# A mixture-of-experts stage: the second product's weights become the moving side, in three passes, and 32 rows of four experts share one pass over column quarters

## The reference

```python
h = jnp.einsum('ech,efh->ecf', buf, expert_w1)
x1, x2 = jnp.split(h, 2, axis=-1)
out = jnp.einsum('ecf,ehf->ech', x1 * jax.nn.silu(x2), expert_w2)
y = out[se, jnp.clip(rank, 0, CAPACITY - 1)]
y = jnp.where(valid[:, None], y * sw[:, None].astype(y.dtype), 0.0)
combined = jnp.zeros((T, H), x.dtype).at[st].add(y)
```

## Time and profile before

| | before |
|---|---|
| median of 3 runs | 1949.8 us (1949.53 to 1949.85) |
| span of the profiled execution | 1947.9 us |
| PE busy over the span | 1899.4 us (98%) |
| DVE, ACT, POOL busy | 1046.4, 829.4, 934.5 us |
| granted clock of PE, mean | 0.989 |
| stage 3 | from about 1238.5 us to the end |

### The profile page before, as it was taken

One profiled execution on the slowest core, in us unless ns is written; L12 is line 12 of the kernel. 1 busy time (PEld: TensorE's weight loads), 2 busy tenths in 40 slices (PEclk: granted clock), 3 DMA queues, 4 the chain that ended last, 5 costly groups with the idle time before them and its releaser, 6 DMA issues.

```text
span 1947.9 us, 35918 instructions
## 1 busy us (share of the span) xinstructions
PE 1899.4 (98%) x12384; PEld 1693.5 (87%) x12384; DVE 1046.4 (54%) x2262; ACT 829.4 (43%) x1661; POOL 934.5 (48%) x667
## 2 busy tenths in 40 slices
PE   7999999999999999999999999889999999999998
PEld 5888888888888887688777887789999999999998
DVE  7877777777777776776667777311221221212211
ACT  6666666666666665553354443111111111211211
POOL 5666666566666662056656666462222222222222
PEclk9999999999999999999999999889999999999999
DMA  6211111111111102121001110567778787787785
GB/s 220 68 37 34 36 33 36 35 45 41 36 36 33 53 11 94 46 75 54 23 23 44 44 33 1 183 177 252 249 258 265 244 272 255 251 273 246 266 266 152
DMA packets 104279, 233.83 MB, mean 120 GB/s; under 512 B 20676, under 2 KB 84891, under 8 KB 96032
## 3 DMA queue, kind: packets, MB, share of 16 engines
q1 hardware_dynamic: 79648, 220.48, 32.4%
q0 software_dynamic: 24576, 12.69, 4.4%
HBM read 194.56 MB, written 78.45 MB: 140 GB/s over the span
## 4 chain that ended last, share of the span: by engine, by line
PE 58%; another core or an unknown queue 1%; DVE 1%; issue 0%; ACT 0%; POOLq 0%; ACTq 0%; POOL 0%; DVEq 0%
PE bank L1870 32%; PE bank L82 19%; PE bank L1149 4%; PE bank L2046 1%; PE bank L2009 1%; PE bank L1647 1%; DVE b_h_low L1429 0%; DVE early L1526 0%; POOLq L2081 0%; DVE c_gT L1965 0%; DVE b_g L1513 0%; DVE b_g L1515 0%; ACT early L1332 0%; ACT b_h_high L1326 0%
## 5 line engine op out<-in xcount | busy, mean ns | idle before, releaser
L1965 DVE TENSOR_TENSOR c_gT<-bank,c_sil 128x480 f32<-128x480 f32 x128 | 84.2, 658 | 559.3 <-PE bank L1870 516.0
L1847 POOL DMA_INDIRECT slots<-b_row,b_index x224 | 249.9, 1116 | 197.8 <-issue 116.3
L1986 POOL DMA_INDIRECT out_rows<-c_y,c_x x96 | 134.2, 1398 | 341.3 <-DMA out_rows<-c_y,c_x 213.7
L1870 PE MATMUL bank<-c_gT,c_w 128*128 128x160 f32 x1536 | 226.9, 304 | 12.4 <-DVE c_gT L1965 10.5
L1870 PEld LDWEIGHTS bank<-c_gT,c_w 128*128 128x128 f32 x1536 | 214.1, 192 | 14.1 <-DVE c_gT L1965 9.3
L1870 PE MATMUL bank<-c_xT,early 128*128 128x160 f32 x1536 | 221.8, 301 | 1.5 <-issue 0.9
L1870 PE MATMUL bank<-c_xT,c_w 128*128 128x160 f32 x1536 | 219.2, 299 | 0.0
L1870 PEld LDWEIGHTS bank<-c_xT,early 128*128 128x128 f32 x1536 | 213.8, 192 | 1.5 <-issue 1.4
L1870 PEld LDWEIGHTS bank<-c_xT,c_w 128*128 128x128 f32 x1536 | 211.4, 190 | 0.0
L1942 ACT ACTIVATE c_sil<-bank 128x480 f32<-128x480 f32 x128 | 73.0, 570 | 287.5 <-PE bank L1870 275.3
L439 POOL TENSOR_TENSOR last_row<-last_row,a_e 128x256 f32<-128x256 f32 x33 | 54.4, 1648 | 129.4 <-DVE a_e L695 127.7
(11 more groups left out here) (317 smaller groups left out, 4940.0 us busy)
## 6 DMA issues: line engine op xcount, KB each, us to landing
c_w<-in_e2T SPq DMA_DIRECT2D x64, 768.0 KB
c_w<-in_e1T SPq DMA_DIRECT2D x32, 1536.0 KB
early<-in_e1T SPq DMA_DIRECT2D x31, 1536.0 KB
slots<-a_fill SPq DMA_DIRECT2D x16, 642.0 KB
c_x<-slots SPq DMA_DIRECT2D x48, 200.6 KB
a_x_in<-in_x SPq DMA_DIRECT2D x32, 128.0 KB, 2.0
xT_tiles<-a_xT SPq DMA_DIRECT2D x32, 128.0 KB
swaT_tiles<-a_swaT SPq DMA_DIRECT2D x32, 128.0 KB
```

The source lines that it names most:

```text
L1847: pool.indirect_dma_start(out=T["slots"], out_offset=bass.IndirectOffsetOnAxis(ap=index[:, t, k:k + 1], axis=0), in_=row[:, t, :], in_offs ...
L1870: return nc.tensor.matmul(out, lhsT, rhs, start=first, stop=last, skip_group_check=True)
L1965: dve.tensor_tensor(flat(gT[p][:, g * H:(g + 1) * H, :]), psum[2 + 2 * g][:, 0:H * CAP], flat(sil[:, g * H:(g + 1) * H, :]), ALU.mult).the ...
L1986: pool.indirect_dma_start(out=T["out"], out_offset=bass.IndirectOffsetOnAxis(ap=token, axis=0), in_=y[q % 2][:, h, :], in_offset=None, bou ...
```

## The change

The edits are all in stage 3, but for one call in stage 2's SP function.

- **Rows.** The 160 rows of an expert are split into a block of 128 (`x`, eight buffers) and a rest of 32 (`x_rest`: the rests of four experts, a quad, stand in the four quarters of one tile's partitions; two such tiles). Their row numbers are loaded once more by themselves (`token_rest`).
- **Second product of the 128 rows.** `gT` is the stationary side now and `w2` moves past it, 256 columns, so that the result has the rows in the partitions, and `yT`, its copies and `turn_y` are gone. It is computed by `mm_split`: ACT makes the high halves of `w2` (1536 columns) and `gT` (twice 384), and DVE the low ones. That is 18 passes of 256 columns.
- **Second product of the rests.** `down_rest` runs once for a quad, as plain float32: for each of 6 slices, four products with 32 stationary columns and 256 moving ones, one for each expert, that write the four quarters of one bank's partitions.
- **Order.** PE's order is `turn_x(n)`, `up` group 1 of n - 1, `up` group 0 of n, `down(n - 1)`, and `down_rest` at every fourth expert. `w2` and `gT` have eight buffers. `w1` and then `w2` of expert n are issued one behind the other, once the first product of expert n - 2 has ended; the rows of expert n wait for the adds of expert n - 8.
- **Adds.** One indirect transfer of 128 rows and one of 32 for each expert; the adds of a quad's first expert wait until the quad's rests are done, which DVE does at the second expert of the next quad.
- **Start and loop.** `first_weights` issues `w1` of experts 0 and 1 and `w2` of expert 0 in stage 2, after its last product with `linT`. POOL issues the 32 scatters that are left in one row ahead of any add. Eight experts are written out ahead of the loop, whose body has eight (6 turns), and eight behind it.

```diff
-    w1 = [buf["early"][:, 0:DC * 2 * FFN].rearrange("p (k f) -> p k f", k=DC), sb("w1_1", [P, DC, 2 * FFN])]
-    w2 = [sb(f"w2_{p}", [P, FC, D]) for p in range(2)]
-    x = [first_rows(buf)] + [sb(f"x{q}", [HALF, 2, ROW])[:] for q in range(1, 4)]
+    w1 = [sb(f"w1_{p}", [P, DC, 2 * FFN]) for p in range(2)]
+    w2_first = sb("w2_0", [P, FC, D])
+    x = [sb(f"x{q}", [P, ROW]) for q in range(RING)]
+    early = [buf["early"][:, p * FC * D:(p + 1) * FC * D].rearrange("p (k d) -> p k d", k=FC) for p in range(2)]
+    w2 = [w2_first[:]] + early + [sb(f"w2_{q}", [P, FC, D])[:] for q in range(3, RING)]
+    w2s = [split(f"w2s{p}", [P, FC, D]) for p in range(2)]
     sil = sb("sil", [P, FC, CAP])
-    gT = [sb(f"gT{p}", [P, FC, CAP]) for p in range(2)]
+    gT = [sb(f"gT{q}", [P, FC, CAP]) for q in range(RING)]
+    gTs = [split(f"gTs{p}", [P, FC, P]) for p in range(2)]
...
+    def experts(eng, step):
+        for n in range(RING):
+            step(n, n, 0)
+        with eng.Fori(1, E // RING - 1) as i:
+            for q in range(RING):
+                step(i * RING + q, q, i)
+        for n in range(E - RING, E):
+            step(n, n % RING, E // RING - 1)
...
+    def first_weights(sp):
+        sp.wait_ge(B("lin_mm"), 4 * CHUNKS)
+        for n in range(2):
+            load_w1(sp, n, n)
+        load_w2(sp, 0, 0)
...
-            wait_past(sp, S("added"), (n - 3) * 32)
+            elif q % QUAD == 0:
+                sp.wait_ge(S("y_rest"), quad_of(q, i) - 1)
+                for j in range(QUAD):
+                    load_rest(n + j, q + j)
+            wait_past(sp, S("added"), (n - RING + 1) * 32)
+            sp.dma_start(x[q][:], slot_rows(T, n, 0, P)).then_inc(S(f"x_in{q}"), 16)
+            sp.dma_start(token_rest[q][:], slot_rows(T, n, P, REST)[:, D + E - 1:ROW]).then_inc(S(f"token_in{q}"), 16)
+            if not first or n >= 2:
+                sp.wait_ge(S("h_mm"), (n - 1) * 4)
+                load_w1(sp, n, q % 2)
+            if not first or n >= 1:
+                if not first:
+                    wait_past(sp, S("rest_mm"), quad_of(q, i) - 1)
+                load_w2(sp, n, q)
...
+        def step(n, q, i):
             p = q % 2
             act.wait_ge(S("xT_mm"), n + 1)
             wait_past(act, S("h_mm"), (n - 1) * 4)
-            act.copy(flat(xT[p][:]), psum[0][:, 0:DC * CAP]).then_inc(S("xT"), 1)
+            by_block = psum[0][:, 0:2 * DC * P].rearrange("p (s k t) -> p s k t", s=2, k=DC)
+            act.copy(xT[p][:, :, 0:P], by_block[:, 0])
+            act.copy(xT[p][:, :, P:CAP], by_block[:, 1, :, quarter(q % QUAD)]).then_inc(S("xT"), 1)
-                   .then_inc(S("sil"), 1)
+                silu(n - 1, 1)
+                g_high(n - 1, (q - 1) % RING, 1)
+            silu(n, 0)
+            act.wait_ge(S(f"w2_in{q}"), (i + 1) * 16)
+            wait_past(act, S("y_mm"), n - 1)
+            act.copy(flat(w2s[p][0][:]), flat(w2[q])).then_inc(S("w2_high"), 1)
+            g_high(n, q, 0)
...
+            dve.wait_ge(S("sil"), 2 * n + g + 1)
+            dve.wait_ge(S("h_mm"), 4 * n + 2 * g + 2)
+            if g == 0 and (not isinstance(n, int) or n >= RING):
+                dve.wait_ge(S("rest_mm"), quad_of(q, i) - 1)
+            dve.tensor_tensor(flat(gT[q][:, g * H:(g + 1) * H, :]), psum[2 + 2 * g][:, 0:H * CAP],
+                              flat(sil[:, g * H:(g + 1) * H, :]), ALU.mult).then_inc(S("gT"), 1)
+        def g_low(n, q, g):
+            part = slice(g * H, (g + 1) * H)
+            dve.wait_ge(S("g_high"), 2 * n + g + 1)
+            low(gTs[q % 2][1][:, part, :], gT[q][:, part, 0:P], gTs[q % 2][0][:, part, :]).then_inc(S("g_low"), 1)
...
+        def step(n, q, i):
+            static = isinstance(n, int)
+            if not static or n >= 2:
+                y_rows(n - 2, (q - 2) % RING)
+            if q % QUAD == 1 and (not static or n > QUAD):
+                rest_rows(n - QUAD - 1, (q // QUAD + 1) % 2, quad_of(q, i) - 1, range(QUAD))
+            if static and n == E - 1:
+                rest_rows(E - QUAD, 1, QUADS - 1, range(0, 2))
+            if not static or n >= 1:
+                before = (i, q - 1) if q else (i - 1, RING - 1)
+                product(n - 1, before[1], before[0], 1)
+                g_low(n - 1, before[1], 1)
+            product(n, q, i, 0)
+            g_low(n, q, 0)
+            dve.wait_ge(S("w2_high"), n + 1)
+            low(flat(w2s[q % 2][1][:]), flat(w2[q]), flat(w2s[q % 2][0][:])).then_inc(S("w2_low"), 1)
...
-            for h in range(2):
-                wait_apart(pool, S("y"), 2 * n + h + 1, S("passed_pool"))
-                token = x[q][:, h, D + E:ROW].bitcast(U32)
-                pool.indirect_dma_start(
-                    out=T["out"], out_offset=bass.IndirectOffsetOnAxis(ap=token, axis=0),
-                    in_=y[q % 2][:, h, :], in_offset=None, bounds_check=last_row, oob_is_err=True,
-                    compute_op=ALU.add).then_inc(S("added"), 16)
+            p, j = q // QUAD, q % QUAD
+            wait_apart(pool, S("y_rest"), groups_of(n) if isinstance(n, int) else quad_of(q, i) + 1, S("passed_pool"))
+            wait_apart(pool, S("y"), n + 1, S("passed_pool"))
+            add(y[q][:], x[q][:, D + E:ROW].bitcast(U32))
+            wait_apart(pool, S(f"token_in{q}"), (i + 1) * 16, S("passed_pool"))
+            add(y_rest[p][quarter(j), :], token_rest[q][:, 1:2].bitcast(U32))
...
-        scatter_rows(pool, T, buf["last_row"], buf["last_index"], (2, 3, 4), last_slot, lambda k: B(f"level{k}"))
+        for k in range(2, TOPK):
+            if k > HELD:
+                scatter_rows(pool, T, row, index, (k,), last_slot, lambda k: B(f"held{k}"))
+            scatter_rows(pool, T, buf["last_row"], buf["last_index"], (k,), last_slot, lambda k: B(f"level{k}"))
...
+        def down(n, p):
+            pe.wait_ge(S("w2_low"), n + 1)
+            wait_past(pe, S("y"), n - 1)
+            for k in range(FC):
+                if k % H == 0:
+                    pe.wait_ge(S("g_low"), 2 * n + k // H + 1)
+                ins = mm_split(nc, psum[Y_BANK[p]][:, 0:D], cut(gTs[p], slice(None), k, slice(None)),
+                               cut(w2s[p], slice(None), k, slice(None)), k == 0, k == FC - 1)
+            ins.then_inc(S("y_mm"), 1)
+        def down_rest(p, group, js):
+            wait_past(pe, S("y_rest"), group)
+            for k in range(FC):
+                for j in js:
+                    q = p * QUAD + j
+                    ins = mm(psum[Y_REST_BANK][quarter(j), 0:D], gT[q][:, k, P:CAP], w2[q][:, k, :],
+                             k == 0, k == FC - 1)
+            ins.then_inc(S("rest_mm"), 1)
+        def step(n, q, i):
+            p = q % 2
+            static = isinstance(n, int)
+            late = not static or n >= 1
+            turn_x(n, q, i)
+            if late:
+                up(n - 1, 1 - p, 1)
+            pe.wait_ge(S(f"w1_in{p}"), (i * (RING // 2) + q // 2 + 1) * 16)
             pe.wait_ge(S("xT"), n + 1)
-            for g in range(2):
+            up(n, p, 0)
+                down(n - 1, 1 - p)
+            if q % QUAD == 0 and (not static or n >= QUAD):
+                down_rest((q // QUAD + 1) % 2, quad_of(q, i) - 1, range(QUAD))
+            if static and n == E - 2:
+                down_rest(1, QUADS - 1, range(0, 2))
...
+        up(E - 1, 1, 1)
+        down(E - 1, 1)
+        down_rest(1, QUADS, range(2, QUAD))
```

More of the change, by code:

```diff
@@ L43 @@
 CAP_B = CAP - P
-HALF = CAP // 2
+QUAD = 4
+RING = 8
+REST = CAP - P
 ROW = D + E + 1
@@ L1970, in vector, with low, product @@
-        experts(dve, step)
-        y_rows(E - 1, 3)
+        def low(out, raw, high):
+            return dve.tensor_tensor(out, raw, high.bitcast(F32), ALU.subtract)
+        def product(n, q, i, g):
+            dve.wait_ge(S("sil"), 2 * n + g + 1)
[4 more added lines that the diff above has]
+                              flat(sil[:, g * H:(g + 1) * H, :]), ALU.mult).then_inc(S("gT"), 1)
@@ L1973, in gpsimd, with add @@
+        experts(dve, step)
+        y_rows(E - 2, RING - 2)
+        product(E - 1, RING - 1, E // RING - 1, 1)
+        g_low(E - 1, RING - 1, 1)
+        y_rows(E - 1, RING - 1)
+        rest_rows(E - QUAD, 1, QUADS, range(2, QUAD))
     def gpsimd(pool):
         last_row = pool.to_reg(TOKENS + CAP - 1)
-        def step(n, q, rows_in, weights_in):
-            if q == 0 and not isinstance(n, int):
+        def add(rows, token):
+            pool.indirect_dma_start(
+                out=T["out"], out_offset=bass.IndirectOffsetOnAxis(ap=token, axis=0),
+                in_=rows, in_offset=None, bounds_check=last_row, oob_is_err=True,
+                compute_op=ALU.add).then_inc(S("added"), 16)
@@ L1979, in step @@
+        def step(n, q, i):
+            if q % QUAD == 0 and not isinstance(n, int):
                 wait_apart(pool, S("added"), n * 32, S("passed_pool"))
@@ L1993, in gpsimd @@
         pool.wait_ge(B("base_out"), 16 * (CHUNKS - 1))
         pool.wait_ge(S("base_out"), 16)
```

(23 more changed lines are left out.)

185 lines of the change are left out of this document (65 added, 120 removed).

## The result

The changed kernel takes 1974.2 us (median of 4 runs, 1972.3 to 1977.4) against 1949.7 of the kernel before on the same chip: a ratio of 1.0129, with a 95% interval of 1.0117 to 1.0141. It is slower by 1.3%; 1907 was forecast. The profiled execution has a span of 1975.7 us.

What follows compares the result with a forecast made beforehand. PE's own work was taken to bound the loop. 1238.5 before stage 3, 616.3 for 64 experts, 33 at the start and 17 at the end made 1904.8 us of span, so 1907 forecast; range 1886 to 1960.

Steps and rivals of the forecast that it cites:

- Adds: Stage 3 loop: adds' turn of 9.7 us at its shortest taken as hidden behind the 9.63 us step; other bound 10.1.
- rival 2: Stage 3 loop: adds and weights in the queue hold the step at 10.1 us, 30 us more, 1937; chance 0.13.
- Second product, transposes, rests, new step: PE's step for one expert: 6.52 + 2.13 + 0.28 + 0.70 = 9.63 us instead of 10.54.
- Rivals 1 and 3: Rests' products on quarters: two at a time, 1948 us, chance 0.17; or one after the other, 2032 us, chance 0.06.
- rival 1: Rests: records start strictly in program order, so only two run at a time; step 10.28 us, total 1948, chance 0.17.
- What hides ACT and DVE: Loop: their work reaches 4.7 and 5.4 us of 9.63; PE covers the 2.3 us chain with 3.26 us.
- Weights: Loop: `w1` has 8.93 us and needs some 6; all transfers fill 8 us, hidden with 1.6 us to spare.
- Start: First experts of stage 3: 33 us lost, from new code beginning in three places; bounds 15 and 80.
- Rival 4: Start of stage 3: new code costs by its length, 80 us and not 33, total 1954; 0.12 including several cases together.
- End: Behind PE's last record: adds of experts 58 to 63 still open, so the span ends some 17 us later instead of 8.

Runs made afterwards that it cites:

- row numbers apart: Changed kernel, but rows wait only for the result of expert n-8, and the adds' row numbers are loaded by themselves two experts later, behind the weights: 1928.9 us.

## Why the prediction was wrong

**The failed step** is "Adds": "weights don't wait behind POOL. I take it as hidden". They do wait: SP's queue is in order, and the wait for `added` stands in front of the weights. The eight buffers weren't slack either. A quad's adds are held until the second expert of the next quad (five experts), and SP runs one and a half ahead, so at the loop's entry the rows of expert 16 had to wait for the adds of expert 8 that POOL had issued four microseconds before (1407.05, SP's rests at 1411.11, its rows at 1416.72). I had written down the turn of adds, 9.7 us "at its shortest" against a step of 9.63, and given the other bound 10.1, for which I had no row; the loop with weights behind the wait has 10.72. This was rival 2, with 0.13, and its 0.47 us for each expert was under half of the 1.06 measured. Its 1937 and the range's upper end of 1960 left out that the adds would then run behind PE.

The sum, term by term, against 1975.7 us of span:

- *Second product, transposes, rests, new step*: 9.66 us measured where nothing else binds, 9.63 forecast. Four quarters run at once (2.80 for 2.8). Over 64 experts 2 us. The Trainium skill's figure of 2.38x for three tiles ("TensorE: Matmul & The Clock Gate", Part 3) would by the prediction's estimate for four have made the quad 3.4 us. The trace has more: 48 records one at a time would need 10.4 us at the 0.216 measured, and 10.4/2.80 is 3.7x. Rivals 1 and 3 are out: the 48 records show four at a time, though the two records of each product want one quarter. The rule of program order, named with rival 1, doesn't hold for these records: strictly in order, as rival 1 worked out, no more than two of them could run side by side.
- *What hides ACT and DVE*: right, no wait for them in the loop.
- *Weights*: their window was enough, as the runs without a bound loop show (PE busy for 100.00 of 100 us without adds and with row numbers apart).
- *Left out of the sum*: 7.8 us. The last quad's rests come in two groups of 2.78 each (2.8 more), each of the first eight experts takes 9.32 where the loop's have 8.89 beside the rests (3.5), and PE waits 0.9 for the last low half and some 0.7 at the first expert.
- *Start*: 32.8 us lost for 33, the right size for a wrong reason. I had counted places where code begins; it is POOL's scatters, 36 in a row by the trace, the 32 among them. That the size came out was luck. Rival 4 falls with the reason. PE also entered stage 3 2.2 us later.
- *The bound loop*: 45.6 us, what is left of PE's end at 1945.0. Of these 42.6 are seen directly: 44 experts from 1423.70 to 1891.31 took 467.6 us where 9.66 each make 425.0.
- *End*: 30.7 us for 17. I had the adds of six experts open 17 us before PE's end, at 5.8 us each. In the trace those of seven hadn't been issued then, five were left at PE's end, and each took 5.5: I had let the adds run at PE's pace until then, and they ran behind it.

1904.8 + 2.2 + 2 + 7.8 + 45.6 + 13.7 = 1976. (The range's lower end, for a start of 15 us, should by the same sum have been 1889 and not 1886.)

## What to carry to other kernels

When a queue's order puts a wait in front of a big transfer, the loop through that wait is a bound of its own: work out its turn with the transfer in it, and compare it with the new step before calling anything hidden; two turns within a few per cent of each other can tip over. Slack in buffers counts from the point at which work is let go, not from the ring's length. And a stall that a change doesn't touch can be the slack that another part lives on: cure it alone, and its gain may be gone.

## What the runs showed of the hardware

- **A burst of scatters slows PE.** After 11 to 14 us of back-to-back indirect transfers from POOL, PE issues one record in some 0.7 to 1.4 us until the burst ends, in new code and in old; 8 in a row cost nothing in these kernels. A burst of 16 cost 4.5 to 13.3 us (8.9 on average), the 36 here 33 us. By what way POOL holds PE up isn't shown; the transfers were nearly idle then (0.12).
- **Two transfers on 64 partitions each are slow.** Cut by halves of the partitions, `w1` made the whole kernel 2128.8 us; cut into every second partition, 1924.6. From 1400 to 1500 the transfers were fuller and moved less, 0.93 and 221 GB/s, where the changed kernel has 0.79 and 261:

```profile
1400.00:1500.00 100.00, 87.96 (x655) 83.73 (x656) 39.81 (x56) 32.10 (x56) 21.37 (x14) 0.91 0.93 221
```

  The Trainium skill ("SBUF — State Buffer", Door 1: The DMA port swizzle) says that partitions 0 to 63 lie on eight of 16 ports and 64 to 127 on the others. The trace agrees: a packet of 12288 B took 0.90 us in the median (1420 to 1860), where it took 0.46 in the changed kernel and with every second partition.
- **Float32 products on four column quarters run side by side.** 48 records of 256 columns took 2.80 us when neighbours differ in their quarter: four start within 0.02 us, the next four 0.216 us behind them. On one quarter each record waits for the one before, 0.216 us as on all columns (0.218).
